# Mixture weights in slots cast in place, the first mixture as one stream of tiles, the second with token-still up products

## What is computed

```
# first mixture: 8 experts, 2 a token, hidden width 1024, and a shared one
probs = softmax(x @ Wg); vals, idx = top_k(probs, 2)
w = vals / (sum(vals) + 1e-9)
y_e = silu(x @ W1[e] + b1[e]) @ W2[e] + b2[e]
out = sum_k w[k] * y_idx[k] + 0.1 * (silu(x @ Ws1 + bs1) @ Ws2 + bs2)

# second mixture: 16 experts, 4 a token by grouped sigmoid routing, width 192
y_e = (silu(x @ w1[e].T) * (x @ w3[e].T)) @ w2[e].T
out = sum_k w[k] * y_idx[k] + shared(x)
```

## Time and profile before

| what | us |
| --- | --- |
| runs | 1731.14, 1715.42, 1727.74; median 1727.74 |
| the profiled execution | 1727.89 |
| its span in the trace | 1725.8 |

### The profile page before, as it was taken

One profiled execution on the slowest core, in us unless ns is written; L12 is line 12 of the kernel. 1 busy time (PEld: TensorE's weight loads), 2 busy tenths in 40 slices (PEclk: granted clock), 3 DMA queues, 4 the chain that ended last, 5 costly groups with the idle time before them and its releaser, 6 DMA issues. The chain is left out here.

```text
span 1725.8 us, 44146 instructions
## 1 busy us (share of the span) xinstructions
PE 1311.5 (76%) x14649; PEld 979.5 (57%) x14649; DVE 1115.8 (65%) x3068; ACT 761.4 (44%) x2055; POOL 466.3 (27%) x495
## 2 busy tenths in 40 slices
PE   4999999977756259769999960999996164988870
PEld 2788888863334249668788850333455034777750
DVE  5899999977999777733433343232257899555646
ACT  6788888854221426633333311511265014444430
POOL 0555555512000210023322200020010125566640
PEclk9999999998887569989999965955598568999985
DMA  3333333310000205511111129068201036222317
GB/s 100 92 76 80 81 77 81 80 56 1 0 1 0 98 27 175 176 45 45 42 42 39 42 86 290 1 219 279 63 1 40 26 111 219 73 89 91 91 61 243
DMA packets 110362, 148.43 MB, mean 86 GB/s; under 512 B 14153, under 2 KB 95506, under 8 KB 110226
## 3 DMA queue, kind: packets, MB, share of 16 engines
q1 hardware_dynamic: 98754, 115.24, 22.0%
q0 software_dynamic: 11328, 30.95, 5.7%
q10 hardware_dynamic: 144, 0.39, 0.1%
HBM read 124.77 MB, written 21.76 MB: 85 GB/s over the span
## 5 line engine op out<-in xcount | busy, mean ns | idle before, releaser
L1177 ACT ACTIVATE _and_attentions_routed_h<-ps,mixture_and_attentions_b 128x128 f32<-128x128 f32 x312 | 89.2, 368 | 162.4 <-PE ps L1130 161.7
L1130 PE MATMUL ps<-xture_and_attentions_x_s,ture_and_attentions_m_wh 128*128 128x128 f16 x1248 | 129.0, 221 | 11.7 <-DVE and_attentions_routed_hs L1215 9.9
L1213 DVE TENSOR_SCALAR and_attentions_routed_hs<-_and_attentions_routed_h 128x512 f16<-128x512 f32 x78 | 33.0, 424 | 150.2 <-PE ps L1143 149.2
L1341 PE MATMUL ps<-stage_second_mixture_x_s,tage_second_mixture_m_wh 128*128 128x128 f16 x948 | 104.6, 228 | 29.2 <-DVE stage_second_mixture_hs L1422 19.9
L641 POOL TENSOR_TENSOR ads_and_recurrence_ctx_s<-ads_and_recurrence_ctx_c,ads_and_recurrence_ctx_s 128x512 f16<-128x512 f32 x64 | 74.2, 1159 | 177.8 <-ACT ads_and_recurrence_ctx_s L570 177.8
L590 ACT ACTIVATE ads_and_recurrence_probs<-ps,s_and_recurrence_neg_max 128x257 f32<-128x257 f32 x256 | 117.8, 480 | 1.1 <-DVE s_and_recurrence_neg_max L672 1.1
L1143 PE MATMUL ps<-ture_and_attentions_m_wh,and_attentions_routed_hs 128*128 x624 | 107.8, 275 | 0.6
L1452 POOL DMA_INDIRECT tage_second_mixture_rows<-n_rows,e_second_mixture_r_token x79 | 85.5, 1082 | 82.2 <-POOLq L899 58.4
L1130 PEld LDWEIGHTS ps<-xture_and_attentions_x_s,ture_and_attentions_m_wh 128*128 x1248 | 93.0, 98 | 23.3 <-issue 13.4
L1456 POOL DMA_INDIRECT y_rows<-stage_second_mixture_y,ge_second_mixture_r_dest x79 | 77.3, 979 | 79.8 <-ACT stage_second_mixture_y L1395 65.3
L1384 ACT ACTIVATE stage_second_mixture_h<-ps 128x256 f32<-128x256 f32 x95 | 36.5, 384 | 140.7 <-PE ps L1341 139.8
(11 more groups left out here) (410 smaller groups left out, 3839.6 us busy)
## 6 DMA issues: line engine op xcount, KB each, us to landing
ads_and_recurrence_ctx_t<-in_ctx_t SPq DMA_DIRECT2D x64, 257.0 KB, 2.7
e_and_attentions_b_ctx_t<-in_ctx_t SPq DMA_DIRECT2D x16, 1028.0 KB, 7.6
xture_and_attentions_raw<-in_m_w SPq DMA_DIRECT2D x32, 512.0 KB, 3.3
ure_and_attentions_b_ctx<-in_ctx SPq DMA_DIRECT2D x32, 512.0 KB
stage_second_mixture_raw<-in_m_w SPq DMA_DIRECT2D x16, 640.0 KB, 4.7
ds_and_recurrence_mask_i<-in_mask SPq DMA_DIRECT2D x256, 32.1 KB, 1.7
stage_second_mixture_c_y<-y_rows SPq DMA_DIRECT2D x16, 512.0 KB, 4.9
xture_and_attentions_c_y<-y_rows SPq DMA_DIRECT2D x16, 256.0 KB, 3.0
```

Source lines behind the costliest of these rows:

```text
L1130: last = pe.matmul(ps[:, UB + 2 * (s % 2) + f // PER, (f % PER) * P:(f % PER + 1) * P], at_block(w, e * mix.blocks + c, f * P, P), a[:, c, :],
L1177: last = act.activation(h32[n][:, at:at + P], ps[:, UB + 2 * (s % 2) + n, at:at + P], ACT.Silu, scale=1 / (WS * NS), bias=b1[:, bass.ds(e ...
L1341: last = pe.matmul(ps[:, UB + u % 4, j * P:(j + 1) * P], at_block(w, e, c * UP + j * P, P), a[:, c, :], start=(n == 0), stop=(n == len(pro ...
```

## The change

1. **Slots.** `wh`, `wl` and the `raw` buffers become one tensor of slots (`Slots`). The raw float32 weights are loaded by four large DMAs on SP at the start of `route`, each into its slot plus two; casting slot i writes the high and low halves, side by side in grains, into slot i. The shared expert comes first in memory.
2. **Early casts.** `route` casts the first 8 slots (first mixture) or 6 (second) on ScalarE and VectorE before the scores are used; GpSimd's casts go. The rest is cast among the shared tiles.
3. **First mixture as one stream.** `first_tiles` runs 16 + 39 tiles in one block. In routed tiles one matmul of 512 columns makes high by high and high by low, and VectorE adds the two halves behind ScalarE's copy. There are three row buffers (R = 3) where there were four; results and turned rows lie in the two free slots.
4. **Experts** are read one tile at a time in the middle of an iteration; a word of six numbers is still loaded every sixth tile.
5. **Second mixture.** Tokens are the still operand of the ascent, 6 matmuls of 384 columns; the hidden rows (tokens on the partitions) are split by three VectorE operations, turned by four transposes (`flip`), copied by ScalarE (`flipped`), and then go down. The order runs one tile further ahead. Results are scaled by VectorE.
6. **Biases** are loaded in the boundary; their own block goes. **Context loads**: two of the five sets stay in the combine, three are issued in the next boundary behind its weights.

```diff
 class Slots:
+    AHEAD = 2
+    def __init__(self, k, mix, ctx):
...
+        self.w = k.sb("m_w", [P, mix.count + self.AHEAD, self.size], F16, ctx=ctx)
+        rest = mix.count - mix.blocks
+        self.ends = [mix.blocks + rest * n // (PARTS - 1) for n in range(PARTS)]
+    def fetch(self, eng):
+        k, first = self.k, 0
+        for part, end in enumerate(self.ends):
+            eng.dma_start(self.w[:, first + self.AHEAD:end + self.AHEAD, :].bitcast(F32), ...).then_inc(k.t_raw[part].sem, 16)
+            first = end
+    def cast_high(self, act, i):
+        k, part = self.k, self.part(i)
+        act.wait_ge(k.t_raw[part].sem, k.t_raw[part].at(1))
+        if i >= self.AHEAD:
+            act.wait_ge(k.t_wlow.sem, k.t_wlow.at(i - self.AHEAD + 1))
+        high, raw = self.split(i, 0), self.raw(i).rearrange("p (b n) -> p b n", n=self.mix.grain)
+        act.activation(high, raw, ACT.Copy, scale=WS).then_inc(k.t_cast.sem, 1)
+    def cast_low(self, dve, i):
+        k = self.k
+        dve.wait_ge(k.t_cast.sem, k.t_cast.at(i + 1))
+        raw = self.raw(i).rearrange("p (b n) -> p b n", n=self.mix.grain)
+        dve.scalar_tensor_tensor(self.split(i, 1), raw, WS, self.split(i, 0), ALU.mult, ALU.subtract).then_inc(k.t_wlow.sem, 1)
```

`PARTS` is 4, so the parts end after 4, 14, 25 and 36 slots (first mixture) and after 1, 6, 11 and 17 (second). In `route`:

```diff
         @block.scalar
         def _(act):
+            for i in range(mix.early):
+                slots.cast_high(act, i)
             scores(act)
         @block.sync
         def _(sp):
-            first = mix.E * mix.blocks
-            for q in range(mix.blocks):
...
+            slots.fetch(sp)
-        @block.gpsimd
...
         @block.vector
...
             dve.tensor_copy(iota_h[:, :], c_["iota"])
+            for i in range(mix.early):
+                slots.cast_low(dve, i)
             choose(dve)
```

In `first_tiles`:

```diff
-    N = NT if shared else mix.tiles
+    N = NT + mix.tiles
+    R = 3
...
-            rows = [k.sb(f"rows{b}", [P, 2 * D], F16, ctx=ctx) for b in range(4)]
+        rows = [k.sb(f"rows{b}", [P, 2 * D], F16, ctx=ctx) for b in range(R)]
...
+                else:
+                    pe.matmul(ps[:, YB + u % 2, 0:2 * D], h, slots.of(e, block, at, 2 * D), start=(f == 0), stop=False)
+                    last = pe.matmul(ps[:, YB + u % 2, 0:D], l, slots.of(e, block, at, D), start=False, stop=(f == FC - 1))
...
+            for u in range(N):
+                if NT <= u + 3 < N:
+                    turn(u + 3)
+                for f in range(FC):
+                    if u + 2 < N:
+                        ascend(u + 2, f)
+                    descend(u, f)
...
+            for u in range(N):
+                if NT <= u + 3 < N:
+                    take(u + 3)
+                if u + 2 < N:
+                    split(u + 2)
+                if u < NT:
+                    add(u)
+                else:
+                    result(u)
+                for i in casts(u):
+                    slots.cast_low(dve, i)
...
             def gather(s):
-                pool.wait_ge(k.t_trans.sem, k.t_trans.at(s - 3))
-                pool.indirect_dma_start(rows[s % 4][:, :], ...
+                pool.wait_ge(k.t_trans.sem, k.t_trans.at(s - R + 1))
+                pool.indirect_dma_start(rows[s % R][:, :], ...
...
+            for s in range(R):
+                gather(s)
+            for s in range(mix.tiles):
+                if s + R < mix.tiles:
+                    gather(s + R)
+                scatter(s)
```

There u counts all tiles, so routed tile s is u = 16 + s. `result(u)` on VectorE waits for ScalarE's copy, adds the second half and releases `scatter`. In `second_tiles`:

```diff
-            def ascend(u, j):
...
+            def ascend(u):
...
+                pe.wait_ge(k.t_gated.sem, k.t_gated.at(u - 1))
+                products = [(w, a, c) for w, a in three((0, 1), x) for c in range(C)]
                 for n, (w, a, c) in enumerate(products):
+                    last = pe.matmul(ps[:, UB + u % 2, 0:UP], a[:, c, :], weight(u, w, c * UP, UP), start=(n == 0), stop=(n == len(products) - 1))
+                last.then_inc(k.t_up.sem, 1)
+            def flip(u):
+                pe.wait_ge(k.t_low.sem, k.t_low.at(u + 1))
+                pe.wait_ge(k.t_hcopied.sem, k.t_hcopied.at(u - 1))
...
+            for u in range(3):
+                ascend(u)
+            flip(0)
             for u in range(N):
+                if NT <= u + 4 < N:
+                    turn(u + 4)
+                if u + 3 < N:
+                    ascend(u + 3)
+                if u + 1 < N:
+                    flip(u + 1)
+                if u + 4 >= NT:
+                    routed.read(u + 4 - NT)
+                descend(u)
...
     def fetch_first(sp):
-        for n in range(A):
+        for n in range(2):
             ring.fetch_turned(sp, n)
             ring.fetch_rows(sp, n)
+    def fetch_others(sp):
+        for n in range(2, A):
```

More of the change, by code:

```diff
@@ L925, in route @@
         iota_h = k.sb("iota_h", [P, P], F16, ctx=ctx)
-        raw = [k.sb(f"shared_raw{p}", [P, mix.width], ctx=ctx) for p in range(2)]
         @block.tensor
@@ L1172, in silu @@
+            def silu(u):
+                e = mix.E if u < NT else routed.of(u - NT)
                 for f in range(FC):
@@ L1448, in _ @@
+                dve.tensor_scalar(y[s % 4][:, :], out, 1 / (WS * HS), None, ALU.mult).then_inc(k.t_ycopied.sem, 1)
+            for u in range(3):
+                multiply(u)
+                high(u)
+                low(u)
+            for u in range(N):
+                if u + 3 < N:
+                    multiply(u + 3)
+                    high(u + 3)
+                    low(u + 3)
+                result(u)
+                for i in casts(u):
+                    slots.cast_low(dve, i)
         @block.gpsimd
```

529 lines of the change are left out of this document (235 added, 294 removed).

## The result

The changed kernel takes 1929.49 us (median of 4 runs, 1929.02 to 1930.05), the kernel before 1729.44 in the same set (4 runs, 1715.42 to 1731.85): ratio 1.118, 95% interval 1.112 to 1.124. The forecast was 1974 us in 1895 to 2055, slower. Its profiled execution took 1930.05 us, its span is 1928.3.

A forecast was written before the change was run, and what follows sets the result against it. TensorE was taken to bound the first mixture's tiles and the second's routed tiles, VectorE the second's shared tiles. 1727.9 + 263 + 24 + 19 - 18 - 42 = 1973.9, say 1974 us; range 1895 to 2055, slower 0.92.

The forecast's parts named there:

- Row ring: First mixture, routed tiles: with three buffers, result, scatter, gather and landing stand in series with TensorE; 7.3 us stall, 35 times.
- Body and clock: First mixture, routed tiles: TensorE's work per tile 5.6 us at full clock, plus 2.1 us lost to low clock per stall.
- The clock term: First mixture: after each stall TensorE restarts at half clock, losing 2.1 us a tile; bounds 0 and 5.6.
- The rival of a clock that stays high: First mixture: no clock loss in the stalls, period 12.9 us, 74 us less, 1900 us; 12 in 100.
- the one that never returns: First mixture: clock never comes back in so short a body, period 18.5 us, 122 us more, 2096 us; 8 in 100.
- The upper bound of this part, +380: First mixture's added time if the whole body of each stalled tile runs at half speed; the lower bound was +187.
- First mixture, sum: Fill, shared tiles, 35 stalled iterations of 15.0 us, four without stall and a tail: 638 against 375.1 us, +263.
- First router: Scores wait for weight loads and eight early casts, read at 616.4 instead of 592.5: +24 us, bounds +8 and +50.
- Second router: Six slots must land and be cast before the scores, 22 us against some 3: +19 us, bounds +8 and +33.
- Context loads: First combine: with only two sets issued there the block ends earlier: -18 us, bounds -20 and -8.
- Second mixture: GpSimd's 130 scatters and gathers bound routed tiles, at most 170 us, after a 54 us start: 224 against 266.1, -42.

The follow-up runs named there:

- The gathers ahead: Changed kernel, still three row buffers, with GpSimd's gathers in the first mixture issued two tiles earlier in its queue: 1601.56 us, ratio 0.936.
- the fillers: Changed kernel with 56 added matmuls, output read by nobody, on TensorE ahead of each stalled turn in the first mixture: 1867.19 us, ratio 1.087.
- all three mended: Changed kernel with gathers issued two tiles earlier, four and one early casts, forty row buffers in the second mixture: 1666.86 us (0.943), again 1582.47 us (0.919).

## Why the prediction was right

*Row ring.* Right in every link: last descent to scatter 3.14 us (forecast 3.15), scatter to gather 1.29 (1.30), landing 2.79 (2.85), a wait of 7.1 (7.3), 35 times. The links are one round's; the 7.1 is the mean of all 35. The gathers ahead took away only the order and all 35 waits went.

*Body and clock.* Body 5.6, as forecast. The clock term was the least supported one, taken from two single pauses of the earlier trace rows. What a wait costs beside its length is 2.1 us by the subtraction above, the very size that I took; but the fillers show that only 1.8 of it is clock. The other 0.3 is in no term of the sum, so that the size came out whole is in part luck. The period goes from 13.8 to 16.3 us, so the loss isn't the same in each round. The Trainium skill, "TensorE: Matmul & The Clock Gate", section on HAM oscillation, says that in a loop which waits for a DMA in each step every step starts cold; the trace agrees: the round shown has its matmuls at half speed after the wait and at full speed later, with a granted clock of 0.73 in the loop and 1.00 with fillers or without waits. The rival of a clock that stays high (1900) and the one that never returns (2096) are both out. (The upper bound of this part, +380, should be +385 by its own terms: 35 x 3.5 more for a period of 18.5.)

*First mixture, sum.* +255.5 for +263: 35 x 0.2 us of wait is 7, and that is the difference.

*First router.* The casts are as late as forecast (scores read at 614.5, forecast 616.4), but the step from there to the end had a fault: I priced the casts taken off GpSimd at nothing, as "off the path", and looked at no row of VectorE beside them. From the scores to the block's end it was 37.3 us before and 29.4 after. The operations of VectorE were slower while GpSimd cast beside them. That is 7.9 of the 9.9 us that the term was too high.

*Second router.* +14.2 for +19, and by the same fault. The scores were read 3.2 us after the block's start before and 21.9 after it in the changed kernel (1580.1 to 1602.05), +18.7 as forecast. From there to the end it was 63.8 us and is 59.3: six operations of VectorE beside GpSimd's casts took 5.72 us before and 1.17 after. So both routers' sums were right where I looked and lacked one term, what GpSimd's casts had cost VectorE.

*Context loads.* -17.5 for -18, and +16.7 in the first instruction's idle time when it was undone (44.9 to 61.6).

*Second mixture.* -50.3 for -42. The routed part was sized right (168.8 for 170 us between first and last scatter). The start was 47 us (1661.3 to the first scatter at 1708.3) where I had 54 (its terms add up to 53): VectorE's cast tiles stood 2.69 us apart where I had 3.0, and the ones behind them 1.3 to 2.1 apart where I had 2.1. In the routed part GpSimd was the bound that I had named, but TensorE's tile took 2.14 us, not 2.05, so that it was no more than level with it.

*What no term held.* Single attention, 11.5 us shorter. Three of fourteen profiles show 99 us, eleven 87 to 88; the kernel before is in both groups, and so is all three mended (87.8, then 99.3). So it belongs to the execution, not to a kernel, and it flattered the change in the comparison of these two profiles. That part of the nearness is luck: without it the change costs 214 us, and the forecast was 32 too high, not 44. The times of the kernel before in the undisturbed sets fall into 1705 to 1719 and 1727 to 1737 in the same way, with none between.

## What to carry to other kernels

Before you take a buffer out of a ring, write the queue of the engine that fills it, and count in iterations what stands before each fill: here three buffers were enough and the place of a gather behind a scatter was not. A wait of some us in each turn of a TensorE loop costs more than its length (2.1 us more for each 7.1 here, 1.8 of them clock), because the clock falls in it; the gain of a mended wait is to be priced with both. And a ring must be compared with the body after the change: a faster body gives its ring less time.

## What the runs showed of the hardware that I had not expected

**VectorE beside GpSimd.** In the first router before, GpSimd cast the shared weights from 593.1 to 610.3 while VectorE worked at small operations. Costliest groups of VectorE in that stretch, kernel before (busy us, then mean ns of one):

```profile
L979 DVE TENSOR_TENSOR xture_and_attentions_tmp<-xture_and_attentions_hot 128x128 f32<-128x128 f32 x1 | 2.1, 2099 | 0.0
L992 DVE TENSOR_SCALAR re_and_attentions_need_i<-ture_and_attentions_upto 128x8 int32<-128x8 f32 x1 | 1.9, 1906 | 0.0
...
L862 DVE CAST _and_attentions_r_choice<-mixture_and_attentions_i 128x128 f32<-128x128 uint32 x1 | 1.1, 1061 | 0.0
```

The same sum of the choices in the changed kernel, where GpSimd rests:

```profile
L1033 DVE TENSOR_TENSOR xture_and_attentions_tmp<-xture_and_attentions_hot 128x128 f32<-128x128 f32 x1 | 0.3, 291 | 0.0
```

2,099 ns against 291; 1,906 ns against 172 and 1,061 against 227 for the other two. The timeline of before shows what these lengths are:

```profile
603.87 2.14 POOL L964 TENSOR_TENSOR ture_and_attentions_m_wl<-nd_attentions_shared_raw,ture_and_attentions_m_wh 128x1024 f16<-128x1024 f32 x1
604.06 2.10 DVE L979 TENSOR_TENSOR xture_and_attentions_tmp<-xture_and_attentions_hot 128x128 f32<-128x128 f32 x1
```

The sum ends 0.15 us after the GpSimd instruction that was under way when it started, and the other two 0.03 and 0.08 after theirs. So each lasted as long as GpSimd's instruction did. The first operation after GpSimd's last cast (ended 610.3) takes its usual 0.28 us again. The Trainium skill, "GPSIMD Engine Reference", section 1, Specifications, says that GpSimd shares its interface to SBUF with VectorE and gets in the way of VectorE instructions in a two-port performance mode or with two inputs in SBUF; the trace agrees for the sum, which has two such inputs. The other two have one, and whether they ran in such a mode no run here shows. Casts on GpSimd were not free: they cost 7.9 us of the first router and 4.5 of the second.

**The clock around attention.** Single attention begins right after projections that run at full clock. The view of stretches, kernel before, then the changed kernel: the 36 us ahead of the first scores, the next 22, and the rest.

```profile
1085.00:1121.00 36.00, 32.96 (x127) 12.71 (x125) 6.89 (x25) 20.21 (x41) 0.70 (x2) 1.00 0.00 1
1121.00:1143.00 22.00, 22.00 (x137) 8.42 (x137) 8.77 (x23) 3.80 (x13) 10.42 (x16) 0.54 0.43 141
1143.00:1219.70 76.70, 76.70 (x421) 29.42 (x424) 18.22 (x63) 11.69 (x43) 0.00 (x0) 0.50 0.84 263
```
```profile
1335.00:1371.30 36.30, 33.26 (x132) 12.84 (x131) 6.89 (x25) 20.27 (x41) 0.78 (x2) 1.00 0.24 75
1371.30:1393.30 22.00, 19.65 (x199) 8.99 (x199) 11.49 (x34) 5.29 (x18) 10.37 (x15) 0.97 0.71 225
1393.30:1458.50 65.20, 65.20 (x362) 24.90 (x365) 15.13 (x53) 10.01 (x36) 0.00 (x0) 0.50 0.89 281
```

The same work meets 0.54 in the one and 0.97 in the other for the first 22 us, 137 matmuls for 199, and 0.50 in both afterwards, though TensorE is busy all the time. Why the clock is held for 22 us longer in most executions, and why it falls with TensorE at work, no run here tells.
